# Moving one chunk's DRAM stores out of the projection stage and the first turn of the maxima forward

## The chip, the cores and the metric

The kernel runs on one core of a Trainium2 chip. The metric is device time in microseconds, the median of three runs. Engines are named as the profile names them: PE (TensorE matmul) and PEld (its weight loads), DVE (VectorE), ACT (ScalarE), POOL (GpSimd), SP (SyncE, which issues the DMAs; SPq is its queue of issues).

## The reference, cut to what matters

The whole program is two layers, each an attention-like block and an expert block. The change touches only the first block, page-masked attention on an input of 4 x 1024 tokens of width 128:

```
q = (x @ wq);  lat = x @ w_down;  k = lat @ wk_up;  v = lat @ wv_up     # 16 heads of 8
q, k = rope(q), rope(k)
scores = q . k / sqrt(8), masked to pages (32 tokens) not later than the query's
out = softmax(scores) @ v @ wo
```

Everything behind it (two expert blocks and a state-space block) is the same in both kernels.

## The kernel before, in words

Work stands in blocks. At the end of a block all engines meet, and none starts the next block before the last has arrived. Two blocks matter: `project_qkv` (line 260) and `attend` (line 505).

`project_qkv` goes over 8 chunks of 512 tokens (4 batches, `CPB` = 2 chunks each). For each chunk PE projects, DVE rotates, and ACT, POOL and DVE split the rotated q and k into three bf16 parts in the tile `parts`, which has two turns. SP then writes them to DRAM as six DMAs (line 294), behind waits on `part_ready`. Each store counts up `written[k]`. From batch 1 on, SP also issues five row loads behind each chunk's stores (line 499, through `load_rows`): the first 25 (`ROWS_BEGUN`) of the 72 loads that fill a ring of four head groups. At the end SP waits for all stores to have landed (line 304).

`attend` works on 16 groups of 4 heads; four groups belong to one batch. A group needs 18 row loads (`ROW_DMAS`), numbered n, so that n = 0 to 17 are group 0's, 18 to 35 group 1's, and so on. For each group:

- PE computes 18 blocks of scores for the row maxima (`maxima(m)`, line 747, `NI` = 18 a group), into two pairs of PSUM banks. DVE reduces each (`take(m)`, line 638), and `maxima(m)` waits for `take(m - 2)`. After a group's last one DVE combines them (lines 650 and 651).
- POOL negates the maxima and splits them into three parts (`negate`, lines 597 to 602).
- PE turns them (`turn`, line 755), ACT copies them to SBUF (line 697), and SP copies them into rows of `qr` (`neg_in_rows`, two DMAs, line 546).
- PE computes the scores with these rows in place (`scores`, line 769), ACT takes the exponent (line 714), and PE multiplies with the values (`values`, line 788).

The maxima run ahead of the scores by `LEAD` blocks. Before the loop PE issues `LEAD` maxima with nothing between them but `turn(0)`; then each of 18 steps of a group issues one maxima block, one pair of scores and the value pieces that are due. `turn(i + 1)` stands in step 14 of group i. `LEAD` was 26, and `turn(0)` stood behind 25 maxima (m = 24).

SP's order in `attend` is a list written by hand: loads n = 25 to 35, then `neg_in_rows(0)`, then loads n = 36 to 71, then `neg_in_rows(1)`, then for each later group its 18 loads, its stores and `neg_in_rows`. The sequencer takes them strictly in this order.

Of the kernel before, what the change touches and what calls it, by code (L numbers as in the profile page):

```python
# [10 lines left out]
BF16 = mybir.dt.bfloat16  # L11
# [4 lines left out]
P = 128  # L16
E = 128
B, T = 4, 1024
N = B * T
NT = N // P  # L20
CH = 512
NCH = N // CH
TPC = CH // P
CPB = T // CH
BANK = 512

H, D = 16, 8
GH = 4
# [226 lines left out]
    return q  # L255


def project_qkv(nc, g, q):

    with ExitStack() as ctx:  # L260
        sb = lambda name, shape, dt=F32: ctx.enter_context(nc.sbuf_tensor(f"qkv_{name}", shape, dt))
        sem = lambda name: ctx.enter_context(nc.semaphore(f"qkv_{name}"))
# [2 lines left out]
        latT = sb("latT", [LAT, 2, CH])  # L265
        by_cos, by_sin, rest = (sb(n, [P, 2, CH]) for n in ("by_cos", "by_sin", "rest"))
        rot = sb("rot", [P, 2, 2, CH])
        parts = sb("parts", [P, 2, 3, 2, CH], BF16)
        lat_done, lat_stored, qk_done, swap_done, v_done, v_stored = map(sem, (
            "lat_done", "lat_stored", "qk_done", "swap_done", "v_done", "v_stored"))  # L270
        cos_taken, swap_taken, rotated, rest_ready = map(sem, ("cos_taken", "swap_taken", "rotated", "rest_ready"))
        part_ready = [sem(f"part_ready{part}") for part in range(3)]
        written = [sem(f"written{k}") for k in range(2)]
        block = ctx.enter_context(nc.Block())
        WRITES = 2 * 3 * 16

        @block.sync
        def _(sp):
            for k in range(2):
                sp.sem_inc(written[k], WRITES)  # L280
            for r in range(2):

                at = HROWS * r + ROWS_QK
                sp.dma_start(g.kr[at:at + 3 + PPB, :, :, :].rearrange("r s p t -> r (s p) t"),
                             g.w["page_k"].rearrange("r (a t) -> r a t", a=1).to_broadcast([3 + PPB, RING * GP, T])).then_inc(g.masks_in, 16)
                sp.dma_start(g.qr[at + 3:at + 3 + PPB, :, :, :].rearrange("r s p t -> r (s p) t"),
                             g.w["page_q"].rearrange("r (a t) -> r a t", a=1).to_broadcast([PPB, RING * GP, T])).then_inc(g.masks_in, 16)
            begun = 0
            for b in range(B):
                for k in range(CPB):  # L290
                    for part in range(3):
                        sp.wait_ge(part_ready[part], part // 2 + CPB * b + k + 1)
                        for which in range(2):
                            sp.dma_start(g.qk_parts[which, part, b * H // GH:(b + 1) * H // GH, :, :, k * CH:(k + 1) * CH].rearrange("g d h t -> (g d h) t"),
                                         parts[:, k, part, which, :]).then_inc(written[k], 16)
                    if CPB * b + k == CPB:
                        for half in range(CPB):
                            sp.wait_ge(written[half], 2 * WRITES)
                    for n in range(begun, min(ROWS_BEGUN, begun + ROWS_A_CHUNK) if b > 0 else 0):
                        load_rows(sp, g, n // ROW_DMAS, n % ROW_DMAS)  # L300
                        begun = n + 1
            assert begun == ROWS_BEGUN
            for k in range(2):
                sp.wait_ge(written[k], WRITES + B * WRITES)

        @block.tensor
        def _(pe):
# [62 lines left out]
        def _(act):  # L370
# [8 lines left out]
            def split(b, k):  # L379
                c = CPB * b + k  # L380
                act.wait_ge(written[k], b * WRITES + WRITES)
                act.wait_ge(rotated, 1 + c + 1)
# [38 lines left out]
GP = GH // 2  # L421
NK = 9
NI = GP * NK
LEAD = NI + 8

# [61 lines left out]
def load_rows(eng, g, i, n):  # L489

    r, run = n % 2, n // 2
    if run == len(ROW_RUNS):
        at = HROWS * r + ROWS_QK
        ins = eng.dma_start(g.qr[at:at + 3, i % RING, :, :], g.w["zero_rows"].rearrange("r (p t) -> r p t", p=GP))
    else:
        which, part, first, count = ROW_RUNS[run]
        at, dst = HROWS * r + first * D, (g.qr, g.kr)[which]
        src = g.qk_parts[which, part, i:i + 1, :, :, :].rearrange("a d (p r) t -> a d p r t", r=2)[:, :, :, r, :]
        ins = eng.dma_start(dst[at:at + count * D, i % RING, :, :], src.to_broadcast([count, D, GP, T]))
    ins.then_inc(g.rows_in[i % RING], 16)  # L500


def attend(nc, g, f):

    with ExitStack() as ctx:
        sb = lambda name, shape, dt=F32: ctx.enter_context(nc.sbuf_tensor(f"att_{name}", shape, dt))
        sem = lambda name: ctx.enter_context(nc.semaphore(f"att_{name}"))
# [28 lines left out]
        @block.sync  # L536
        def _(sp):
            def store(i):
                sp.wait_ge(out_stored, i + 1)
                sp.dma_start(g.heads[GH * i:GH * (i + 1), :, :, :].rearrange("h k r t -> (h k r) t"), out_sb[:, i % 2, :]).then_inc(out_written[i % 2], 16)  # L540

            def neg_in_rows(i):
                sp.wait_ge(neg_stored, i + 1)
                for r in range(2):
                    at, rows_of = HROWS * r + ROWS_QK, 3 * GP * NJ
                    sp.dma_start(qr[at:at + 3, i % RING, :, :].rearrange("r p t -> r (p t)"),
                                 neg_rows[rows_of * r:rows_of * (r + 1), :]).then_inc(neg_in, 16)

            for n in range(ROWS_BEGUN, RING * ROW_DMAS):
                load_rows(sp, g, n // ROW_DMAS, n % ROW_DMAS)  # L550
                if n == 2 * ROW_DMAS - 1:
                    neg_in_rows(0)
            for i in range(NG):
                if i >= 1 and i + RING - 1 < NG:
                    sp.wait_ge(scores_done, UNITS * i)
                    for n in range(ROW_DMAS):
                        load_rows(sp, g, i + RING - 1, n)
                if i == LOADS_AT:
                    sp.dma_start(f.wo[:, :], g.w["wo"]).then_inc(f.wo_in, 16)
                    for group in (f.e.route, f.e):  # L560
                        for dst, src in group.pairs:
                            sp.dma_start(dst, src).then_inc(group.loaded, 16)
                if i == NG - 1:
                    f.store_inverses(sp, 2)
                    f.load_heads(sp, 2)
                if i >= 1:
                    store(i - 1)
                for b in range(3):
                    if i == SUMS_AT[b]:
                        f.load_sums(sp, b)  # L570
                for b in range(EARLY):
                    if i == INVERSES_AT[b]:
                        f.store_inverses(sp, b)
                    if i == HEADS_AT[b]:
                        f.load_heads(sp, b)
                if i < NG - 1:
                    neg_in_rows(i + 1)
            f.store_row_tables(sp, 0)
            store(NG - 1)
# [152 lines left out]
        def _(pe):  # L732
# [3 lines left out]
            def maxima(m):  # L736

                i, (pair, item) = m // NI, divmod(m % NI, NK)
                if m % NI == 0:
                    pe.wait_ge(rows_in[i % RING], ROW_LOADS * (i // RING + 1))  # L740
                if m >= 2:
                    pe.wait_ge(max_taken, m - 1)
                at = 0
                for q_block, key, n, diagonal in MAXIMA[item][0]:
                    count = ROWS_D if diagonal else ROWS_QK
                    for r in range(2):
                        last = pe.matmul(PS[:, MAX_BANK + 2 * (m % 2) + r, at:at + n], rows(qr, count, i, pair, r, q_block * P, P),  # L747
                                         rows(kr, count, i, pair, r, key, n), start=True, stop=True)
                    at += n
                last.then_inc(max_scores_done, 1)  # L750
# [40 lines left out]

            for m in range(LEAD):
                maxima(m)
                if m == LEAD - 2:
                    turn(0)
            for i in range(NG):
                for k in range(NK):
                    for pair in range(GP):
                        ahead = LEAD + NI * i + GP * k + pair
                        if ahead < NG * NI:  # L800
# [652 lines left out]
def attention(nc, g, q, f):  # L1453

    with ExitStack() as ctx:
        g.V = ctx.enter_context(nc.sbuf_tensor("V", [P, B * 4, T // P, 32], F32))
        g.qr, g.kr = (ctx.enter_context(nc.sbuf_tensor(n, [P, RING, GP, T], BF16)) for n in ("qr", "kr"))
        g.masks_in = ctx.enter_context(nc.semaphore("masks_in"))
        g.rows_in = [ctx.enter_context(nc.semaphore(f"rows_in{r}")) for r in range(RING)]
        project_qkv(nc, g, q)  # L1460
        attend(nc, g, f)
# [831 lines left out]
```

## Time and profile before

| | |
|---|---|
| median of three runs | 1396.83 us (1396.3 to 1397.82) |
| the profiled execution: time, span | 1397.44 us, 1395.6 us |
| mean granted TensorE clock | 0.937 of full |
| PE busy | 1230.7 us (88%) |
| DVE busy | 1090.8 us (78%) |
| ACT busy | 851.2 us (61%) |
| POOL busy | 574.8 us (41%) |
| `project_qkv` | about 28 to 92 us of the span |
| `attend` | about 92 to 499 us of the span |

The profile is of one execution, whose time is 0.6 us above the median and 1.8 us above its own span. Times in the rows are microseconds from the start of the span; "idle before" and its releaser stand in brackets. Matmuls are pipelined and their ends are modelled, so starts are the safer reading.

### The profile page before, as it was taken

How to read it: one execution, taken by the hardware profiler on the slowest of the kernel's cores; microseconds unless marked ns; L12 is line 12 of the kernel's file. 1: busy time of each engine (PE TensorE's matmuls, PEld its weight loads, DVE VectorE, ACT ScalarE, POOL GpSimd, SP SyncE). 2: the span in 40 equal slices, each digit the busy share in tenths (PEclk: the TensorE clock that was granted, in tenths of full speed). 3: DMA queues.
4: the chain of work that ended last, by engine and by line, in shares of the span. 5: the costliest groups of instructions: out<-in, count | busy, mean ns of one | idle time of the engine just before them, and what ended most of it. 6: DMA issues, size and time to landing. Idle time of an engine off the chain costs nothing. (4 is left out here: it accounts for less than half of the span.)

```text
span 1395.6 us, 23364 instructions
## 1 busy us (share of the span) xinstructions
PE 1230.7 (88%) x8438; PEld 643.8 (46%) x8438; DVE 1090.8 (78%) x1318; ACT 851.2 (61%) x1506; POOL 574.8 (41%) x428
## 2 busy tenths in 40 slices
PE   4936999999899989989996866999999999976998
PEld 2411333334333434444543334555555556564665
DVE  5768999989799555867455766999999999864554
ACT  2523899989799742222222678989999899512221
POOL 2320010000100236656665114888888888820000
PEclk9965999999999999999997897999999999985999
DMA  4331111311211165323361001223232223101231
GB/s 111 113 115 31 55 60 48 104 56 55 75 54 50 41 93 143 114 91 113 103 116 23 0 5 49 93 94 100 91 103 94 91 94 103 61 29 24 60 62 38
DMA packets 70525, 103.16 MB, mean 74 GB/s; under 512 B 12598, under 2 KB 42246, under 8 KB 70422
## 3 DMA queue, kind: packets, MB, share of 16 engines
q1 hardware_dynamic: 69126, 100.47, 25.1%
q10 hardware_dynamic: 1296, 1.33, 0.4%
q8 instruction: 64, 1.05, 0.3%
q14 instruction: 39, 0.32, 0.1%
HBM read 88.00 MB, written 13.37 MB: 73 GB/s over the span
## 5 line engine op out<-in xcount | busy, mean ns | idle before, releaser
L638 DVE TENSOR_REDUCE att_found<-PS 128x2 f32<-128x1024 f32 (+2 forms) x288 | 333.2, 1218 | 20.9 <-PE PS L747 19.0
L714 ACT ACTIVATE att_prob<-PS 128x512 f32<-128x512 f32 x576 | 313.6, 596 | 46.1 <-PE PS L769 34.4
L1930 POOL TENSOR_TENSOR ms_ch<-xnT,ms_c_rows 128x1024 f32<-128x1024 f32 x103 | 243.7, 2367 | 45.4 <-PE PS L1840 33.3
L1840 PE MATMUL PS<-ms_ch,ident_sb 128*128 128x512 f32 x512 | 241.2, 593 | 1.0 <-POOL ms_ch L1930 1.0
L1891 DVE TENSOR_TENSOR_SCAN xnT<-xnT,PS 128x1024 f32<-128x1024 f32 x103 | 231.0, 2267 | 7.2 <-PE PS L1831 7.1
L1869 ACT ACTIVATE ms_scaled<-m_dtu_turns,m_bt 128x256 f32<-128x256 f32 x448 | 191.6, 495 | 29.3 <-PE PS L1831 29.3
L788 PE MATMUL PS<-att_prob,att_v 128*32 128x256 f32 (+1 forms) x2560 | 185.0, 376 | 2.8 <-ACT fr_out L703 2.6
L1831 PEld LDWEIGHTS PS<-ident_sb,ms_scaled 128*128 128x128 f32 x1024 | 119.3, 142 | 81.4 <-DVE xnT L1891 37.9
L747 PE MATMUL PS<-kr,qr 55*128 55x128 bf16 (+4 forms) x1152 | 121.7, 293 | 31.0 <-PEq L260 15.8
L1831 PE MATMUL PS<-ident_sb,ms_scaled 128*128 128x128 f32 x1024 | 135.4, 276 | 11.1 <-ACT ms_scaled L1869 5.6
L1262 ACT ACTIVATE f_h<-PS,e_w_b 128x512 f32<-128x512 f32 x64 | 44.0, 687 | 140.1 <-PE PS L1413 136.9
L769 PE MATMUL PS<-qr,kr 55*128 55x128 bf16 (+4 forms) x1152 | 115.6, 279 | 15.7 <-ACT att_prob L714 8.3
L1840 PEld LDWEIGHTS PS<-ms_ch,ident_sb 128*128 128x128 f32 x512 | 87.3, 190 | 64.6 <-issue 61.2
L1876 ACT ACTIVATE xnT<-m_dt,m_a 128x1024 f32<-128x1024 f32 x103 | 116.9, 1136 | 0.0
L747 PEld LDWEIGHTS PS<-kr,qr 48*128 48x128 bf16 (+1 forms) x1152 | 39.8, 97 | 138.7 <-issue 90.6
L1243 POOL TENSOR_TENSOR f_yT<-f_yT,f_prod 128x512 f32<-128x512 f32 x56 | 71.0, 1267 | 71.6 <-DVE f_prod L1355 70.3
L1345 DVE SCALAR_TENSOR_TENSOR f_x3s<-PS,e_w_b,f_mask_row 128x512 f32<-128x512 f32 x64 | 48.0, 749 | 61.5 <-PE PS L1417 60.8
L1231 POOL TENSOR_TENSOR f_xm<-xnT,f_gate_row 128x512 f32<-128x512 f32 x64 | 81.2, 1269 | 15.7 <-DMA f_gate_row<-gate_rows_dram 14.0
L788 PEld LDWEIGHTS PS<-att_prob,att_v 128*32 128x32 f32 x2560 | 55.2, 109 | 63.2 <-issue 53.9
L1422 PE MATMUL PS<-f_h,e_w_w 128*128 128x512 f32 x128 | 67.1, 606 | 8.5 <-DVE f_prod L1355 8.4
L1413 PE MATMUL PS<-f_xm,e_w_w 128*128 128x512 f32 x128 | 68.2, 615 | 5.7 <-POOL f_xm L1231 5.7
L2165 ACT ACTIVATE f_sg<-PS 128x512 f32<-128x512 f32 x40 | 23.9, 597 | 78.7 <-PE PS L2148 78.7
(225 smaller groups left out, 1724.9 us busy)
## 6 DMA issues: line engine op xcount, KB each, us to landing
ms_c_rows<-bc_rows_dram SPq DMA_DIRECT2D x64, 512.0 KB, 3.7
f_gate_row<-gate_rows_dram SPq DMA_DIRECT2D x64, 256.0 KB, 3.5
f_mask_row<-mask_rows_dram SPq DMA_DIRECT2D x64, 128.0 KB, 3.1
qk_parts_dram<-qkv_parts SPq DMA_DIRECT2D x48, 128.0 KB, 1.9
heads_dram<-fr_out SPq DMA_DIRECT2D x16, 256.0 KB, 3.0
f_mask_row<-mask_rows_dram SPq DMA_DIRECT2D x64, 64.0 KB, 3.2
qr<-qk_parts_dram SPq DMA_DIRECT2D x32, 96.0 KB
qr<-qk_parts_dram SPq DMA_DIRECT2D x96, 32.0 KB
```

What stands on the lines that cost most here:

```text
L638: dve.tensor_reduce(found[:, :, pair, first:first + (n - 1) * step + 1:step], PS[:, bank:bank + 2, :].rearrange("p r (w n) -> p r w n", w= ...
L714: act.activation(prob[:, step % PROB_RING * GH + h, :], PS[:, SCORE_BANK + unit % SCORE_RING, :], ACT.Exp, scale=float(D) ** -0.5).then_in ...
L747: last = pe.matmul(PS[:, MAX_BANK + 2 * (m % 2) + r, at:at + n], rows(qr, count, i, pair, r, q_block * P, P), rows(kr, count, i, pair, r, ...
L769: last[r] = pe.matmul(PS[:, SCORE_BANK + (unit + r) % SCORE_RING, col:col + w], rows(kr, count, i, pair, r, j * P, P), rows(qr, count, i, ...
L788: last = pe.matmul(PS[VW * h:VW * (h + 1), VALUE_BANK, q - half * CH:q - half * CH + w], v1[:, i % 2, half, h, j, :], prob[:, step % PROB_ ...
L1231: pool.tensor_tensor(xm[:, e % XM_RING, :], xnT[:, c * CH:(c + 1) * CH], gate_row[:, e % ROW_RING, :], ALU.mult).then_inc(xm_ready, 1)
L1831: last = pe.transpose(PS[:, X_BANK + 2 * half + k // TPC, k % TPC * P:(k % TPC + 1) * P], scaled[:, s % 2, k, half, :], g.ident[:, :])
L1840: last = pe.matmul(PS[:, Y_BANK + 2 * half + q, :], g.ident[:, :], ch[:, half, q * CH:(q + 1) * CH], start=n == 0, stop=n == NS - 1)
L1869: last = act.activation(scaled[:, s % 2, i, :, :], m.dtu_turns[:, TB * b + i, :, :], ACT.Identity, scale=m.bt[:, at:at + 1])
L1876: act.activation(decay_then_h(s, half), m.dt[:, half, sequence(b)], ACT.Exp, scale=m.a[:, half, n:n + 1]).then_inc(decay_ready, 1)
L1891: dve.tensor_tensor_scan(decay_then_h(s, half), decay_then_h(s, half), inputs(half), 0.0, ALU.mult, ALU.add).then_inc(scanned, 1)
L1930: pool.tensor_tensor(ch[:, half, :], decay_then_h(s, half), c_rows[:, s % C_RING, :], ALU.mult).then_inc(ch_ready, 1)
```

## The change

The last chunk's six stores leave `project_qkv`. They are issued in `attend`, by SP, behind load n = 35 and ahead of `neg_in_rows(0)`. The wait for all stores moves to SP's place ahead of the loads of group 4 (the first of batch 1). For that, `parts` and two sets of semaphores now live through both blocks. Second, `turn(0)` stands behind 21 maxima (m = 20) in place of 25, and `LEAD` is 24 in place of 26.

```
+WRITES = 2 * 3 * 16
+def write_parts(queue, g, b, k):
+    for part in range(3):
+        queue.wait_ge(g.part_ready[part], part // 2 + CPB * b + k + 1)
+        for which in range(2):
+            queue.dma_start(g.qk_parts[which, part, b * H // GH:(b + 1) * H // GH, :, :, k * CH:(k + 1) * CH].rearrange("g d h t -> (g d h) t"),
+                            g.parts[:, k, part, which, :]).then_inc(g.written[k], 16)
 # project_qkv, SP
-                    for part in range(3):
-                        sp.wait_ge(part_ready[part], part // 2 + CPB * b + k + 1)
-                        for which in range(2):
-                            sp.dma_start(...).then_inc(written[k], 16)
+                    if CPB * b + k < NCH - 1:
+                        write_parts(sp, g, b, k)
-            for k in range(2):
-                sp.wait_ge(written[k], WRITES + B * WRITES)
 # attend
-LEAD = NI + 8
+LEAD = NI + 6
 # attend, SP
                 if n == 2 * ROW_DMAS - 1:
+                    write_parts(sp, g, B - 1, CPB - 1)
                     neg_in_rows(0)
             for i in range(NG):
                 if i >= 1 and i + RING - 1 < NG:
                     sp.wait_ge(scores_done, UNITS * i)
+                    if i == 1:
+                        for k in range(CPB):
+                            sp.wait_ge(g.written[k], WRITES + B * WRITES)
 # attend, PE
             for m in range(LEAD):
                 maxima(m)
-                if m == LEAD - 2:
+                if m == NI + 2:
                     turn(0)
```

## Rows read from the trace of the kernel before

**Rows 1.** Timeline, all engines, 76 to 93 us: start, length, what, idle before
```profile
77.84 0.75 SPq L494 DMA_DIRECT2D qr<-zero_rows  x2
...
83.53 3.49 SPq L499 DMA_DIRECT2D qr<-qk_parts_dram  x5
83.57 1.22 DVE L350 TENSOR_TENSOR qkv_parts<-qkv_rest,qkv_parts 128x1024 bf16<-128x1024 f32 x1 [4.24 <-ACT qkv_parts L388]
87.07 2.88 SPq L294 DMA_DIRECT2D qk_parts_dram<-qkv_parts  x6
91.84 0.66 SPq L499 DMA_DIRECT2D qr<-qk_parts_dram  x1
...
92.04 1.04 PE L747 MATMUL PS<-kr,qr 48*128 48x384 bf16 x8 [15.81 <-PEq L260]
```

**Rows 2.** Waits of SP's queue, 57 to 93 us: total, times, longest
```profile
SPq L304 <- DMA qk_parts_dram<-qkv_parts: 1.4, 1, 1.4
```

**Rows 3.** Timeline of the stretch before the first scores, 92 to 124 us
```profile
92.76 20.45 DVE L638 TENSOR_REDUCE att_found<-PS 128x2 f32<-128x1024 f32 x18 [0.65 <-PE PS L747]
...
114.91 0.61 PE L747 MATMUL PS<-kr,qr 48*128 48x512 bf16 x2 [1.03 <-DVE att_found L638]
114.98 0.24 POOL L602 TENSOR_TENSOR att_neg_parts<-att_neg_rest,att_neg_parts 128x32 bf16<-128x32 f32 x1
...
119.43 0.61 PE L747 MATMUL PS<-kr,qr 55*128 55x128 bf16 x6 [0.53 <-DVE att_found L638]
...
119.97 0.34 PE L755 MATMUL PS<-identb_sb,att_neg_parts 128*96 128x128 bf16 x1
...
120.65 1.56 SPq L546 DMA_DIRECT2D qr<-att_neg_rows  x2
...
122.25 5.68 SPq L499 DMA_DIRECT2D qr<-qk_parts_dram  x8
...
123.81 0.61 PE L769 MATMUL PS<-qr,kr 55*128 55x128 bf16 x4 [1.51 <-DMA qr<-att_neg_rows]
```

**Rows 4.** Timeline at the start of group 1, 144 to 150 us
```profile
144.38 0.27 ACT L697 ACTIVATE att_neg_rows<-PS 96x128 bf16<-96x128 bf16 x1
...
146.85 1.54 SPq L546 DMA_DIRECT2D qr<-att_neg_rows  x2
...
149.94 0.40 PE L769 MATMUL PS<-qr,kr 55*128 55x128 bf16 x4 [1.56 <-DMA qr<-att_neg_rows]
```

**Rows 5.** Timeline of a later group, 161 to 184 us
```profile
161.85 0.22 DVE L650 TENSOR_REDUCE att_row_max<-att_found 128x16 f32<-128x64 f32 x1
...
163.58 0.24 POOL L602 TENSOR_TENSOR att_neg_parts<-att_neg_rest,att_neg_parts 128x32 bf16<-128x32 f32 x1
...
167.31 0.26 PE L755 MATMUL PS<-identb_sb,att_neg_parts 128*96 128x128 bf16 x1
...
183.38 0.22 DVE L650 TENSOR_REDUCE att_row_max<-att_found 128x16 f32<-128x64 f32 x1
```

**Rows 6.** Timeline where the maxima end, group 14, 452 to 454 us
```profile
452.28 0.39 PE L769 MATMUL PS<-qr,kr 51*128 51x512 bf16 x2
...
453.36 0.39 PE L769 MATMUL PS<-qr,kr 55*128 55x128 bf16 x4
```

**Rows 7.** Waits of DVE over all of attention, 92 to 500 us
```profile
DVE att_found L638 <- PE PS L747: 19.0, 25, 4.9
```

**Rows 8.** Timeline of PE: two steps at 130 us, one restart at 282
```profile
129.53 1.08 PE L788 MATMUL PS<-att_prob,att_v 128*32 128x256 f32 x8
...
131.51 1.08 PE L788 MATMUL PS<-att_prob,att_v 128*32 128x256 f32 x8
...
281.71 0.61 PE L769 MATMUL PS<-qr,kr 55*128 55x128 bf16 x4 [1.66 <-DMA qr<-att_neg_rows]
```

**Rows 9.** Windows: length, busy PE, PEld, DVE, ACT, POOL, clock, DMA share, GB/s
```profile
134.00:135.00 1.00, 1.00 (x16) 0.38 (x8) 0.40 (x1) 0.68 (x2) 0.00 (x0) 0.56 0.23 74
...
284.00:286.00 2.00, 2.00 (x28) 0.69 (x30) 1.51 (x2) 1.19 (x3) 0.00 (x0) 0.73 0.19 60
```

More of the change, by code:

```diff
@@ L267, in project_qkv @@
         rot = sb("rot", [P, 2, 2, CH])
-        parts = sb("parts", [P, 2, 3, 2, CH], BF16)
+        parts, part_ready, written = g.parts, g.part_ready, g.written
         lat_done, lat_stored, qk_done, swap_done, v_done, v_stored = map(sem, (
@@ L271, in project_qkv @@
         cos_taken, swap_taken, rotated, rest_ready = map(sem, ("cos_taken", "swap_taken", "rotated", "rest_ready"))
-        part_ready = [sem(f"part_ready{part}") for part in range(3)]
-        written = [sem(f"written{k}") for k in range(2)]
         block = ctx.enter_context(nc.Block())
-        WRITES = 2 * 3 * 16
         @block.sync
@@ L290, in _ @@
                 for k in range(CPB):
-                    for part in range(3):
-                        sp.wait_ge(part_ready[part], part // 2 + CPB * b + k + 1)
-                        for which in range(2):
-                            sp.dma_start(g.qk_parts[which, part, b * H // GH:(b + 1) * H // GH, :, :, k * CH:(k + 1) * CH].rearrange("g d h t -> (g d h) t"),
-                                         parts[:, k, part, which, :]).then_inc(written[k], 16)
+                    if CPB * b + k < NCH - 1:
+                        write_parts(sp, g, b, k)
                     if CPB * b + k == CPB:
@@ L1457, in attention @@
         g.qr, g.kr = (ctx.enter_context(nc.sbuf_tensor(n, [P, RING, GP, T], BF16)) for n in ("qr", "kr"))
+        g.parts = ctx.enter_context(nc.sbuf_tensor("parts", [P, 2, 3, 2, CH], BF16))
+        g.part_ready = [ctx.enter_context(nc.semaphore(f"part_ready{part}")) for part in range(3)]
+        g.written = [ctx.enter_context(nc.semaphore(f"written{k}")) for k in range(2)]
         g.masks_in = ctx.enter_context(nc.semaphore("masks_in"))
```

## The prediction

> **What bounds the kernel now.** I read the page first: PE is busy for most of the span, and the chain that ended last lies at the far end, in the last block. So nothing there is touched, and a gain in attention counts in full only if the stages behind it simply move forward. They do, as far as they wait for attention as a whole: all engines meet at its end. So the question is what ends attention, and I went on to the timeline of the two places that the diff edits, then the waits of SP and DVE, then one group in the middle, then the clock.
>
> At the seam between projection and attention nothing computes. DVE's last work ends at 84.79 (83.57 + 1.22), SP issues five loads up to 87.02, then the last chunk's six stores up to 89.95, and attention begins at 91.84 [rows 1]. SP's wait for the landing is 1.4 us [rows 2], so that it is over at 91.35; the meeting of the engines takes the other 0.49.
>
> Before the first scores DVE sets the pace: 18 reductions in 20.45 us, one every 1.13 (17 x 1.13 + 1.23), while PE waits between its blocks [rows 3]. POOL has the negated maxima ready at 115.22 (114.98 + 0.24), but PE turns them only at 119.97, because its order puts 25 maxima ahead. SP issues the copy into the rows at 120.65, and the scores start at 123.81, having waited 1.51 for it [rows 3]. DVE needs to have done no more for this than group 0's maxima.
>
> From group 1 on, a group takes 21.53 us (183.38 - 161.85) [rows 5]. DVE's own work in it is 18 x 1.13 + 0.4 = 20.7, so PE's order sets the pace, and DVE has 0.8 to spare. One irregular place matters. At the start of group 1 the rows were copied by ACT at 144.65 (144.38 + 0.27), yet SP issues their DMAs at 146.85, since it was still busy with loads n = 36 to 71, which stand behind `neg_in_rows(0)` in its order; PE stands idle for 1.56 us until 149.94 [rows 4].
>
> **The change part by part.**
>
> *Stores out of the projection.* SP's last work there becomes the five loads that end at 87.02; every other engine is through by 84.79. With the same 0.49 for the meeting, attention begins at 87.51 in place of 91.84: 4.33 us less. Below: if the meeting is dearer when nobody has waited long, 4.0. Above, the meeting could cost nothing: 4.8. The six stores do not vanish: 2.88 us of issuing on SP behind n = 35. In attention SP issues n = 25 to 35 in about 7.2 us (eleven at 0.66 as the one in [rows 1]), to 94.7, the stores to 97.6, and then waits for the turned maxima until about 111.8. So they lie in the shade of the first maxima. Group 1's rows stand ahead of the stores, and are issued by 94.7 against their first use after 18 maxima, about 107.9. Group 0's last loads were issued at 78.59 (77.84 + 0.75) [rows 1], nine us before the new start. The new wait for the stores stands about 50 us behind their issue: nothing. Its price without that cover would be a landing, the 1.4 of [rows 2].
>
> *The turn behind m = 20.* On the axis of before, `maxima(20)` starts at 114.91 and POOL is through at 115.22 [rows 3]. Behind `maxima(24)`, PE came to the turn 0.54 after that block's start (119.43 to 119.97); the same here gives 115.45, so neither waits much for the other. That is 4.52 us earlier. SP's copy goes out 0.68 behind the turn, at 116.13 instead of 120.65, and the scores may start 3.16 behind that, at 119.29.
>
> *LEAD 24.* The block ahead of the first scores is now m = 24, which waits for DVE until 119.43 as before [rows 3]. The scores follow 0.54 later, at 119.97. So the first scores move by 3.84 us, and the copy lands 0.68 before they can use it. DVE loses its short idle time there, and so nothing is shifted onto it.
>
> *What the start of group 1 makes of it.* There SP decides, not PE. From the copy of group 0 to that of group 1 SP has 26.20 us of issuing (120.65 to 146.85), and the scores follow 3.09 after [rows 3, 4]. All of this hangs on the first copy, so group 1 starts 4.52 earlier, not 3.84: PE's idle 1.56 us shrinks to 0.88. ACT's copy would be there at 140.81, well ahead of SP at 142.33, so SP still decides. If it did not, only the 3.84 would hold.
>
> *What LEAD costs later.* Two maxima blocks leave the stretch where DVE sets the pace and go into the loop. Every step up to step 9 of group 14 issues one block as before; steps 10 and 11 of that group get one that they lacked. A step without one takes 1.08 us there (452.28 to 453.36) [rows 6], against 1.20 on average with one, turn and values included (21.53 / 18). So it costs between nothing (ACT's exponents fill most of such a step anyway) and 0.24; I take 0.1, since a plain step differs less than the mean does.
>
> *The slack of the negation.* A group's last reduction now comes two steps later, while the turn stays. Today combining starts at 161.85, POOL ends at 163.82 (163.58 + 0.24), 1.97 later, and the turn is at 167.31 [rows 5]: 3.49 to spare. Two steps are 2.26 at 1.13, so 1.2 stay. Nothing is lost, but most of the cushion is used up.
>
> Sum: 4.33 + 4.52 - 0.1 = 8.75 us. The profiled execution's span would be 1395.6 - 8.75 = 1386.85, its time 1388.7. The median of before is 0.6 below that execution, so 1396.83 - 8.75 = 1388.1.
>
> **The clock.** A cold step takes 1.98 us (129.53 to 131.51) [rows 8] at the lower level of 1.2 GHz, against the 1.20 warm: 0.39 us lost per cold us. The clock came back to 2.4 GHz late in the us 134 to 135 (mean 0.56) [rows 9], 11 us after the first scores, of which PE was dense only from 129.53. After 281.71 it came back within 3.5 us (the stretch 284 to 286 has 0.73) [rows 8, 9]. So the rise should move with the work, give or take 2 us, 0.8 us of time. Because SP sets the start of group 1, the first 0.88 us lost by PE ahead of it is free. Farther on there is luck: PE's stall of 1.66 us before 281.71 met a falling clock, the one of 1.56 before 149.94 did not. Such a fall costs about 3.5 x 0.39 = 1.4. That makes a spread of about 1.5 to both sides.
>
> The Trainium skill's page "TensorE: Matmul & The Clock Gate", Part 1, says that activity is judged in windows that run freely and don't restart with a kernel's work, so that the moment of the rise varies with where the work falls in them. The two unequal delays fit it, and it is the mechanism of the second rival.
>
> **The rivals.**
>
> 1. *Forecast*: both gains hold, 1388.1. For it: each term is a gap with a named cause. Chance 0.73, with its own range 1386.0 to 1390.0.
> 2. *The clock rises no earlier*. The rise stays at about 134.9 while the work comes 8.2 earlier. PE loses 8.2 x 0.39 = 3.2, of which 0.88 is free, so 2.3: 1390.4. Against it: the restart at 281.71. By the page's rule this is a matter of phase and would be partial. Chance 0.09.
> 3. *DVE becomes the bound*. Attention can't be shorter than DVE's chain of reductions. It idles 19.0 us over attention [rows 7] and has 0.8 us more in each group, and the forecast asks for only 2.2 less: its first reduction comes 4.33 earlier, its last 8.75 - 2.26 = 6.5. If the small slack in a group is no slack, only the 4.33 and the DVE idle time at the first scores, about 1, come: 1391.5. Chance 0.06.
> 4. *The change doesn't do what it says at the seam*: what holds attention back until 91.84 is something else, or the meeting waits for outstanding DMAs of the block by itself. Then only the 4.42 of the turn stays: 1392.4. Chance 0.05.
> 5. *Slower*: the negation misses its turn in each group, since its cushion is down to 1.2 us. PE would stand for each us that it is later, 14 times. It decides from a lateness of 1.2 + 8.75 / 14 = 1.8 us; at 2 us late, 14 x 0.8 = 11.2 is lost against 8.75 won: 1399.3. Against it: POOL's chain takes 1.97 in [rows 5], and in the first group 2.01 from the last reduction's end at 113.21 to 115.22 [rows 3]. Chance 0.03.
> 6. *Better luck with the clock*, the fall at 282 gone and the first rise early: 1386 or less. Chance 0.04.
>
> A difference under 0.2% (2.8 us) is about what can't be told from no change. Forecast, 2, 3, 4 and 6 are all faster by more than that: 0.96 with a little taken off, since a partial 4 with bad luck in the clock lands within it. Same 0.02, slower 0.03. The range from 1385.6 to 1392.0 takes in the forecast, the clock's luck on both sides and cases 2 and 3 with the spread of the runs; outside lie 4, 5 and the ends.
>
> **What the profile after would show.** The first matmul of line 747 at about 87.7; stores of line 294 (or of the new helper) on SP between 94 and 98; the first turn 23.6 us behind attention's start (before 28.1); the first scores 28.1 after it (before 32.0), without a wait for the row copy; PE's wait for `att_neg_rows` at the start of group 1 about 0.9; a group's period still 21.5; POOL's last negation 1.2 us ahead of the turn. The prediction is wrong if attention starts later than 88, if PE's turn waits for POOL in every group, or if the clock's rise does not move.

## The result, and the profile after

The changed kernel takes 1386.23 us (median of six runs, 1382.46 to 1388.82) against 1396.37 us for the kernel before in six runs (1393.34 to 1397.82): a ratio of 0.9934, interval 0.9915 to 0.9952. Forecast was 1388.1, or 8.75 us less than the 1396.83 of the first three runs; the medians of six differ by 10.1. Measured again later, the same pair gave 0.9913 (0.9887 to 0.9938). Six runs of one kernel spread over 4 to 10 us, and 35 runs of the kernel before over nearly 16, so single terms of the sum can't be read from run times. They can be read from the profiles, where the intervals inside attention that the order of issue fixes repeat to 0.1 us. The rest of the program does not repeat as well: from the end of attention to the end of the span the fourteen profiles have 890.0 to 895.9 us (895.9 and 894.7 in the first pair).

Timeline of the changed kernel at the seam (start, length, what, idle before); it answers to [rows 1]:

```profile
84.60 4.88 SPq L503 DMA_DIRECT2D qr<-qk_parts_dram  x6
84.93 1.23 DVE L354 TENSOR_TENSOR parts<-qkv_rest,parts 128x1024 bf16<-128x1024 f32 x1 [4.54 <-ACT parts L392]
88.83 0.12 POOL L591 MEMSET att_zero<- 128x32 f32 x1 [5.02 <-POOLq L272]
...
89.02 1.04 PE L755 MATMUL PS<-kr,qr 48*128 48x384 bf16 x8 [11.72 <-PEq L272]
...
96.09 2.79 SPq L266 DMA_DIRECT2D qk_parts_dram<-parts  x6
```

Attention starts 3.9 us behind the start of DVE's last work (88.83 - 84.93), before 8.28 (91.85 - 83.57). The six stores are at 96.09, in the shade of the first maxima. The group of six loads that starts at 84.60 includes the first one of attention. The fifth, the last of the projection, ends at 88.09, so the meeting of the engines takes 0.74 us here (88.83 - 88.09), where the forecast took 0.49. Everything up to here lies 1.1 to 1.4 us later than in the profile before, work that the change doesn't touch, so in what follows times are counted from attention's start.

Timeline up to the first scores, answering to [rows 3]:

```profile
89.74 20.46 DVE L646 TENSOR_REDUCE att_found<-PS 128x2 f32<-128x1024 f32 x18 [0.65 <-PE PS L755]
...
111.89 0.61 PE L755 MATMUL PS<-kr,qr 48*128 48x512 bf16 x2 [1.03 <-DVE att_found L646]
111.97 0.25 POOL L610 TENSOR_TENSOR att_neg_parts<-att_neg_rest,att_neg_parts 128x32 bf16<-128x32 f32 x1
...
112.43 0.34 PE L763 MATMUL PS<-identb_sb,att_neg_parts 128*96 128x128 bf16 x1
...
113.11 1.55 SPq L550 DMA_DIRECT2D qr<-att_neg_rows  x2
...
116.82 0.63 PE L777 MATMUL PS<-qr,kr 55*128 55x128 bf16 x4
```

The turn comes 0.54 behind its maxima block, 0.21 behind POOL's end (112.22), and 23.60 us after the start: the forecast's number. The scores start at 27.99 without a wait, forecast 28.1.

Timeline at the start of group 1, answering to [rows 4]:

```profile
138.40 0.27 ACT L705 ACTIVATE att_neg_rows<-PS 96x128 bf16<-96x128 bf16 x1
138.52 0.75 SPq L498 DMA_DIRECT2D qr<-zero_rows  x2
...
139.31 1.53 SPq L550 DMA_DIRECT2D qr<-att_neg_rows  x2
...
142.34 0.39 PE L777 MATMUL PS<-qr,kr 55*128 55x128 bf16 x4
```

The second copy goes out 26.20 us behind the first (139.31 - 113.11), as before, 4.52 us earlier counted from the start. But PE's wait for it is gone where 0.88 was forecast: the clock rose 13.3 us after the first scores and not 11.1, so PE came later. The window in which it rose (length, busy PE, PEld, DVE, ACT, POOL, clock, DMA, GB/s):

```profile
130.00:131.00 1.00, 1.00 (x16) 0.26 (x14) 0.83 (x1) 0.50 (x2) 0.00 (x0) 0.94 0.34 74
```

A later group, timelines of DVE, POOL and PE, answering to [rows 5]:

```profile
178.04 0.22 DVE L658 TENSOR_REDUCE att_row_max<-att_found 128x16 f32<-128x64 f32 x1
...
179.79 0.25 POOL L610 TENSOR_TENSOR att_neg_parts<-att_neg_rest,att_neg_parts 128x32 bf16<-128x32 f32 x1
...
181.25 0.26 PE L763 MATMUL PS<-identb_sb,att_neg_parts 128*96 128x128 bf16 x1
...
199.57 0.22 DVE L658 TENSOR_REDUCE att_row_max<-att_found 128x16 f32<-128x64 f32 x1
```

A group still takes 21.53, and POOL ends 1.21 us ahead of the turn, where the forecast said 1.2.

Attention as a whole took 402.01 us, from 88.83 to the first load of the expert block at 490.84; before, 407.83. That is 5.8 less, and the forecast had 4.4. The first profile pair shows one place that was not forecast. PE's wait of 1.66 us at the start of group 7, at whose end the clock fell [rows 8, 9], is down to a quarter of a microsecond:

```profile
272.26 0.39 PE L777 MATMUL PS<-qr,kr 55*128 55x128 bf16 x4 [0.24 <-DMA qr<-att_neg_rows]
```

From the copy for group 7 to that for group 8 it is 24.49 us before and 21.04 after. The other way, the last group of the changed kernel met a clock at half speed from about 461 to 471. Behind its last row copy attention takes 40.8 us, in the kernel before 38.4, so this cost some 2.4 us. Whether such places belong to a kernel or to one execution, one pair of profiles can't tell.

### The profile page after: what moved, and what is told of

It reads as the page before. It is cut to its first block and busy times, and to the rows that moved or that the text cites. A ratio compares the mean times of both kernels' runs of the same rounds, so it can differ in the third digit from the quotient of the medians.

```text
span 1385.5 us, 23363 instructions
## 1 busy us (share of the span) xinstructions
PE 1233.7 (89%) x8438; PEld 647.1 (47%) x8438; DVE 1089.5 (79%) x1318; ACT 851.2 (61%) x1506; POOL 575.9 (42%) x428
## 3 DMA queue, kind: packets, MB, share of 16 engines
q8 instruction: 64, 1.05, 0.3%
## 5 line engine op out<-in xcount | busy, mean ns | idle before, releaser
L777 PE MATMUL PS<-qr,kr 55*128 55x128 bf16 (+4 forms) x1152 | 116.0, 279 | 10.3 <-ACT att_prob L722 7.4
L1239 POOL TENSOR_TENSOR f_xm<-xnT,f_gate_row 128x512 f32<-128x512 f32 x64 | 81.2, 1271 | 11.4 <-DMA f_gate_row<-gate_rows_dram 7.5
L605 POOL TENSOR_TENSOR att_neg<-att_zero,att_row_max 128x32 f32<-128x32 f32 x16 | 4.1, 254 | 164.7 <-DVE att_row_max L659 164.7
```

Of the source, the lines that this page charges most:

```text
L777: last[r] = pe.matmul(PS[:, SCORE_BANK + (unit + r) % SCORE_RING, col:col + w], rows(kr, count, i, pair, r, j * P, P), rows(qr, count, i, ...
L1239: pool.tensor_tensor(xm[:, e % XM_RING, :], xnT[:, c * CH:(c + 1) * CH], gate_row[:, e % ROW_RING, :], ALU.mult).then_inc(xm_ready, 1)
```

## The experiments

Eight further kernels ran, and four of the ten were run once more. The table gives what thirteen of the profiles show, in us; that of e5_lead22 is told under its run. Seam: from the start of DVE's last work in the projection to attention's start. First turn, first scores, copy 0 and copy 1 (the row copies of groups 0 and 1) are counted from attention's start. Wait: PE's wait for copy 1. Rise: from the first scores to the return of the clock to 2.4 GHz. Length: of attention, to the first load of the expert block.

| kernel | seam | turn | scores | copy 0 | copy 1 | wait | rise | length |
|---|---|---|---|---|---|---|---|---|
| before | 8.28 | 28.1 | 32.0 | 28.80 | 55.00 | 1.56 | 11.1 | 407.83 |
| b_again | 8.19 | 28.1 | 31.9 | 28.80 | 55.01 | 2.67 | 8.9 | 407.96 |
| e1_stores_only | 4.08 | 28.2 | 31.9 | 28.84 | 55.06 | 2.42 | 9.3 | 407.58 |
| e3_lead_only | 7.89 | 25.9 | 29.6 | 26.53 | 52.74 | 2.01 | 10.3 | 404.43 |
| e4_turn_only | 6.84 | 23.6 | 30.2 | 24.27 | 50.87 | none | 10.4 | 401.82 |
| e2_turn_lead_only | 7.95 | 23.6 | 28.0 | 24.27 | 50.48 | 0.88 | 11.5 | 400.53 |
| after | 3.90 | 23.6 | 28.0 | 24.28 | 50.48 | none | 13.3 | 402.01 |
| a_again | 3.72 | 23.6 | 28.0 | 24.28 | 50.50 | 1.97 | 8.9 | 401.37 |
| e6_rows20 | 1.51 | 23.6 | 28.0 | 24.27 | 50.67 | none | 15.2 | 400.47 |
| e6_again | 1.52 | 23.6 | 28.0 | 24.27 | 50.50 | 0.94 | 11.4 | 400.39 |
| e7_copy_ahead | 4.41 | 23.6 | 28.0 | 24.28 | 50.70 | none | 15.3 | 403.90 |
| e8_both | 1.51 | 23.6 | 28.0 | 24.28 | 48.25 | 0.68 | 9.5 | 401.41 |
| e8_again | 1.52 | 23.6 | 28.0 | 24.28 | 49.87 | none | 13.3 | 399.86 |

### One half of the change at a time

**e1_stores_only**, the changed kernel with the old lead and the old place of the turn:

```
-LEAD = NI + 6
+LEAD = NI + 8
-                if m == NI + 2:
+                if m == LEAD - 2:
                     turn(0)
```

> Only the last chunk's stores are moved (LEAD 26, first turn behind m = 24, as before). Two separate gaps: attention begins 4.1 to 4.4 us sooner behind the projection's last DVE work (before: 8.27 us behind its start, now 3.9), nothing changes inside attention: first turn 28.1 us and first scores 32.0 us after attention's start, 1.5 us idle for the row copy at the start of group 1. Time 4.3 us under before (1392). Rival, one gap gives the room for the other (part of the gain is only there with both): under 3 us or over 6 us. If the stall of 1.7 us at the start of group 7 depends on the order of maxima, it is still there in this kernel; if it is a matter of how the weight loads fall, it may be there or not.

Measured: 1390.2 us (12 runs), ratio 0.997 (0.9949 to 0.9991) to the kernel before on its chip, 3.7 us less by the medians. The seam is 4.08 and attention as long as before. So the seam's gain stands alone. The start of group 7 waited for only 0.22 us here, with LEAD 26. PE's timeline at the start of group 1, and the clock behind it:

```profile
147.36 0.50 PE L777 MATMUL PS<-qr,kr 55*128 55x128 bf16 x4 [2.42 <-DMA qr<-att_neg_rows]
```

```profile
147.00:148.00 1.00, 0.64 (x8) 0.31 (x12) 0.00 (x0) 0.06 (x1) 0.00 (x0) 0.76 0.11 41
148.00:149.00 1.00, 1.00 (x10) 0.13 (x4) 0.00 (x0) 1.00 (x2) 0.00 (x0) 0.50 0.23 74
```

The clock had risen early here (9.3), PE then waited longer, 2.42 us, and the clock fell behind the wait.

**e2_turn_lead_only**, the kernel before with the other half:

```
-LEAD = NI + 8
+LEAD = NI + 6
-                if m == LEAD - 2:
+                if m == NI + 2:
                     turn(0)
```

> Only the turn and the lead are changed; the stores stay in the projection. Separate gaps: attention begins as before (8.3 us behind the start of DVE's last work), the first turn comes 23.6 us and the first scores 28.0 us after attention's start, group 1's scores 53.6 us after it (before 58.1), time 4.4 us under before (1392). If LEAD 24 also takes away the stall of 1.7 us at the start of group 7 and the fall of the clock behind it, attention is shorter by 5.8 us as in the changed kernel, and the time is 5.8 under (1390.5). Rival, DVE bound: under 1.5 us.

Measured: 1388.92 us (12 runs), ratio 0.9965 (0.995 to 0.9981), 5.0 us less. Turn, scores and copy 1 are as in the changed kernel to 0.02 us, group 1's scores come 53.62 us after the start, forecast 53.6. Attention is 7.3 us shorter than in the first profile of the kernel before. DVE is not the bound. e1's and e2's ratios leave 0.3% and 0.35%, and the whole change 0.66% and 0.87% in its two measurements: the halves add up within what the runs can tell.

**e3_lead_only**, the kernel before with `LEAD = NI + 6` and the turn still behind `LEAD - 2`:

> Only LEAD is 24; the first turn stands behind m = 22 by the old rule LEAD - 2. The turn comes two reductions sooner, 25.9 us after attention's start, the scores 3.8 us behind it, 29.7, with about 1.5 us idle for the row copy, and group 1's scores 2.3 us sooner: 2.2 us under before (1394.2). If the stall at group 7 goes away by LEAD alone, it is absent here and the time is about 3.6 under (1392.8).

Measured: 1391.24 us (12 runs), ratio 0.9978 (0.9962 to 0.9994), 2.7 us less. Turn 25.86, scores 29.63, copy 1 2.27 us sooner than before, as expected; attention is 3.1 to 3.5 us shorter. The expectation asked whether LEAD alone takes the wait at group 7 away: it is still there with 1.12 us, but without a fall of the clock.

**e4_turn_only**, the kernel before with the turn behind `m == NI + 2` and LEAD still 26:

> Only the first turn is put behind m = 20; LEAD stays 26. The turn comes 23.6 us after attention's start, but the scores stand behind m = 26, which waits for DVE: 30.4 us after the start (1.6 sooner). Group 1's scores come 3.1 us sooner, since SP's row copy no longer holds them. Time 3.1 us under before (1393.3). Rival, what counts is when the scores begin, and SP's loads don't matter: 1.6 us. The stall at group 7 is there as before if it depends on the order of maxima.

Measured: 1389.93 us (12 runs), ratio 0.9974 (0.9955 to 0.9994), 4.0 us less. The turn is at 23.60 and the scores at 30.24 (expected 30.4). The interval between the copies is 26.60 here, more than SP's 26.20, so PE and ACT set it, and PE does not wait at all for the copy. Group 1's scores come 54.44 us after the start (147.54 - 93.10), 3.65 sooner than before, where 3.1 was expected. Attention is 401.82 us long, 6.0 under the first profile. The rest of that is not the turn's doing: the first profile had no fall of the clock at group 1, but one at group 7, and from copy 6 to copy 8 it has 47.10 us against 44.75 here. Against b_again and e1 it is the fall at group 1 that is gone with the wait: from copy 1 to copy 2 they have 23.92 and 22.51, e4 21.53. In what the order of issue fixes, the first turn alone brings 3.65 of the 4.5 us that turn and lead bring together.

### How much room the lead has

**e5_lead22**, the changed kernel with `LEAD = NI + 4`:

> The changed kernel with LEAD 22 in place of 24. Theory, the cushion of 1.2 us between POOL's last negation and the turn is what limits LEAD: the last reduction of a group comes 2.26 us later still, so the turn stands 1.05 to 1.2 us for POOL in each of 14 groups, a group takes 22.6 us in place of 21.5, and the time is some 13 to 16 us over the changed kernel (about 1400). Rival, there is more room (DVE is ahead there, or PE's waiting is won back by its next steps): within 2 us of the changed kernel.

Measured: 1424.19 us (6 runs), ratio 1.0199 (1.0172 to 1.0226) to before. The changed kernel was not measured beside it; at its two ratios it would take 1382 to 1385 us, so this is some 40 us over it. The direction is that of the theory (13 to 16 us over), the size nearly three times its own. DVE's timeline of two combinings, PE's at the turn between them, and two windows of the clock behind the turn:

```profile
234.34 0.22 DVE L658 TENSOR_REDUCE att_row_max<-att_found 128x16 f32<-128x64 f32 x1
...
236.47 0.23 PE L763 MATMUL PS<-identb_sb,att_neg_parts 128*96 128x128 bf16 x1 [1.51 <-POOL att_neg_parts L610]
...
258.87 0.22 DVE L658 TENSOR_REDUCE att_row_max<-att_found 128x16 f32<-128x64 f32 x1
```

```profile
238.00:239.00 1.00, 1.00 (x16) 0.57 (x16) 0.74 (x2) 0.66 (x2) 0.00 (x0) 0.63 0.05 12
239.00:240.00 1.00, 1.00 (x18) 0.58 (x18) 0.77 (x1) 0.97 (x2) 0.00 (x0) 0.50 0.14 29
```

PE stands for POOL's negation for 1.51 us in each group, and a group takes 24.53 us in place of 21.53. The expectation had the wait at 1.05 to 1.2. Another 1.5 us go with the clock, which falls behind the wait. Two steps of lead fewer turn a cushion of 1.21 us into a loss of 3.0 us per group.

### Two steps further

**e6_rows20**, the changed kernel with the last five row loads taken out of the projection too:

```
-ROWS_BEGUN = ROWS_A_CHUNK * (NCH - CPB - 1)
+ROWS_BEGUN = ROWS_A_CHUNK * (NCH - CPB - 2)
```

> The changed kernel, and the five row loads n = 20 to 24 leave the projection too (ROWS_BEGUN 20). Theory, what ends the projection now is only SP's list: then the next in line is DVE's last work, and attention begins 1.7 to 2.0 us behind that work's start in place of 3.9, 2 us sooner; inside attention nothing changes, since SP's list of 16 loads and 6 stores (about 13.6 us) still ends before the first copy at 24.3. Time 2 us under the changed kernel. Rival, the meeting of the engines or a landing holds it at 3.9: no gain. Rival, group 1's loads come too late for the 19th maxima block (21 us after the start): a stall of DVE there.

Measured: 1383.81 us (6 runs), ratio 0.9927 (0.9902 to 0.9952) to before on its chip. Timeline at the seam:

```profile
84.26 1.23 DVE L354 TENSOR_TENSOR parts<-qkv_rest,parts 128x1024 bf16<-128x1024 f32 x1 [4.40 <-ACT parts L392]
85.76 4.20 SPq L503 DMA_DIRECT2D qr<-qk_parts_dram  x6
85.77 0.12 POOL L591 MEMSET att_zero<- 128x32 f32 x1 [2.63 <-POOLq L272]
...
85.96 1.03 PE L755 MATMUL PS<-kr,qr 48*128 48x384 bf16 x8 [9.19 <-PEq L272]
```

DVE's last work ends at 85.49, and attention starts 0.28 behind it. Inside attention the first turn, the first scores and copy 0 didn't move.

**e7_copy_ahead**, the changed kernel with the copy of group 1 ahead of SP's last four loads:

```
                     neg_in_rows(0)
+                if n == RING * ROW_DMAS - 5:
+                    neg_in_rows(1)
...
-                if i < NG - 1:
+                if 0 < i < NG - 1:
                     neg_in_rows(i + 1)
```

> The changed kernel, and SP issues the row copy of group 1 ahead of the last four of the loads n = 36 to 71. Theory, SP's list sets the start of group 1 (26.20 us from the first copy to the second in five kernels of this study): the copy now goes out as soon as ACT has it or 2.9 us sooner, whichever is later; with the clock's rise as in the changed kernel that is 0.6 us sooner, with an early rise up to 1.5. So the interval shrinks from 26.20 to between 23.3 and 25.8, and the time by 0.5 to 1.5 us. Rival, the interval is set by PE and ACT: nothing.

Measured: 1385.11 us (6 runs), ratio 0.9927 (0.99 to 0.9954). The changed kernel was not measured beside it, and the profile doesn't decide: the clock rose 15.3 us after the first scores, and SP stood for ACT's copy, so that the interval was 26.42 us.

**e8_both**, both edits:

> Both of these edits on top of the changed kernel: rows n = 20 to 24 moved and the copy of group 1 ahead of four loads. Separate gaps: 2 us from the seam and 0.5 to 1.5 at the start of group 1, 2.5 to 3.5 us under the changed kernel (about 1383 against 1386 on the same chip), attention's start 1.7 to 2.0 behind the start of DVE's last work in the projection.

Measured: 1381.84 us (6 runs), ratio 0.9906 (0.9879 to 0.9934). With an early rise (9.5) the interval between the copies is 23.97 us, so SP's list is what had set 26.20. But the scores gain less, as SP's and PE's timelines show:

```profile
134.73 1.48 SPq L550 DMA_DIRECT2D qr<-att_neg_rows  x2
...
139.03 0.39 PE L779 MATMUL PS<-qr,kr 55*128 55x128 bf16 x4 [0.68 <-DMA qr<-att_neg_rows]
```

The scores follow 4.30 us behind the issue of the copy, where it was 3.03 to 3.16 in the rows above. Why this landing is later was not tried. It is not peculiar to e8: at group 7 the scores follow the issue of the copy by 5.08 us in the first profile of the kernel before and by 4.43 in e4, PE waiting for the landing both times.

### The same kernels again, on one chip

**a_again**, **b_again**, **e6_again** and **e8_again** are the changed kernel, the kernel before, e6_rows20 and e8_both without an edit.

> The changed kernel once more, for its time beside the two below on one chip and for a second profile. Inside attention the first turn 23.6 us, the first scores 28.0 and the second row copy 50.5 us after the start are fixed by the order of issue and come out again within 0.1; what follows the clock may differ: its rise 9 to 15 us after the first scores, and the wait for the row copy at group 7 between 0 and 2 us. If the long wait at group 7 in the kernel before (1.66 us, with a fall of the clock, 3.1 us in all) is chance, the median gain over many runs is near 8.7 us and not the 10 of the two profiles.

> The kernel before once more, for a second profile. First turn 28.1, first scores 32.0, second row copy 55.0 us after attention's start again; attention begins 7 to 8.3 us behind the start of DVE's last work in the projection. If group 7's long wait was chance, the interval between its row copies is now about 21.1 to 22.5 in place of 24.5, and attention 3 us shorter than in the first profile. If it belongs to the kernel, 24.5 comes again.

> The kernel with five more row loads out of the projection (ROWS_BEGUN 20), beside the changed kernel on one chip: attention's start again 1.5 us behind the start of DVE's last work (3.9 to 4.4 in the changed kernel), the time 2.4 us less.

> Both edits, beside the changed kernel on one chip: 2.4 us from the seam, and at the start of group 1 between 0 and 1.5 us, since the first look showed the copy going out at 24.0 us behind the first in place of 26.2, but PE still waiting 0.7 us for it. Time 2.4 to 3.5 us less than the changed kernel.

Measured against 1394.9 us for the kernel before: a_again 1384.28 (0.9913, 0.9887 to 0.9938), b_again 1393.12 (0.9994, 0.9975 to 1.0014), e6_again 1380.6 (0.9898, 0.987 to 0.9926), e8_again 1382.38 (0.9901, 0.9876 to 0.9926). Everything that the order of issue fixes came again within 0.1 us, the seam within 0.2. Copy 1 of e6 and e8 is not of that kind: where the clock rose late SP stood for ACT's copy, and e8 has 48.25 and 49.87. The gain of the changed kernel did not shrink to the 8.7 us that a_again expected: the medians differ by 10.6. e8_again is 1.9 us under the changed kernel, where 2.4 to 3.5 was expected.

Group 7 was chance: b_again shows 21.49 us between the copies for groups 7 and 8 where the first profile had 24.49. But b_again is no shorter than the first profile, since its PE waited 2.67 us at group 1 and the clock fell at the end of that wait. The interval from copy 1 to copy 2 was 23.92 us, against 21.06 in the first profile.

The profiles also show what the chance is. SP's list sets the start of group 7 too, since the weight loads for later blocks stand in it ahead of that group's row copy. From the first of them (`fr_wo`) to the copy SP took 7.2 to 9.0 us, because one or two of these loads, mostly done in 0.5, held it longer, a single one for up to 3.4. In the nine profiles with LEAD 24 PE's wait follows this length: none at 7.23 to 7.36, 0.24 and 0.34 at 7.66 and 7.55, then 0.73 at 8.09, 0.91 at 8.29, 1.12 at 8.50 and 1.60 at 8.99. That last one is e8_both, in which the clock fell at group 7 as it had in the kernel before. SP's timeline of its three `e_w_sw` loads:

```profile
261.06 4.29 SPq L572 DMA_DIRECT2D e_w_sw<-sw  x3
```

In the kernel before the list was short (7.47), and the wait of 1.66 came from the late landing told above.

The order of maxima does matter in one way, which all profiles of the table agree on. At group 6, DVE has 0.95 us of another work, the reciprocal that divides batch 0, right behind a combining. PE's wait for DVE there, in the kernel before:

```profile
271.96 0.39 PE L747 MATMUL PS<-kr,qr 48*128 48x512 bf16 x2 [0.72 <-DVE att_found L638]
```

and in the changed kernel:

```profile
266.62 0.39 PE L755 MATMUL PS<-kr,qr 48*128 48x512 bf16 x2 [0.32 <-DVE att_found L646]
```

With LEAD 26 it is 0.72 or 0.73 (before, b_again, e1, e4), with LEAD 24 0.32 or 0.33 (all others). From copy 6 to copy 8, less the wait at group 7, it is 43.8 to 44.0 us with LEAD 26 (b_again, e1, e4) and 43.4 to 43.6 in the eight profiles with LEAD 24 in which the clock did not fall there.

The reciprocal of batch 1, in group 10, shows the same 0.72 and 0.32, but a few microseconds on PE stands much longer, in every profile of the table, for 4.2 to 5.4 us. In the kernel before:

```profile
370.59 0.31 PE L755 MATMUL PS<-identb_sb,att_neg_parts 128*96 128x128 bf16 x1 [4.60 <-POOL att_neg_parts L602]
```

POOL negates late here because it first divides batch 0, and that waits for the DMA into `fr_inv` (until 365.28); the clock is down there for 3.4 to 10.2 us. The change leaves this place as it was, and no run here tried it.

e6 is the fastest in the median on the last chip, 3.7 us under the changed kernel, and 2.2 us of that are the seam (3.72 to 1.52). The intervals of e6, e8 and the changed kernel overlap, so only the profiles, not the times, say that e6 is faster; between e6 and e8 nothing is decided.

## Why the prediction was right

**The seam.** Forecast 4.33. In five profiles with the stores in the projection the seam is 6.84 to 8.28 (mean 7.83), in five that differ from the changed kernel only inside attention (e1, e5, e7 and its own two) 3.72 to 4.41 (mean 4.06): 3.8 us, and 4.4 in the first pair. e1 shows that it comes from the stores alone, and e6 that the five loads were next in line, as the forecast had read them. The fourth rival (something else holds the start) is out. The meeting of the engines is not one number: it costs 0.28 where DVE came last (e6) and 0.74 where SP did (the changed kernel), and the forecast took 0.49. By its letter one of the forecast's signs of being wrong came true, since attention starts at 88.83, later than 88. But DVE's last work starts 1.36 later in that profile, and counted from it the start is at 3.90, forecast 3.94.

**The turn and the lead.** Forecast: turn at 23.6, scores at 28.1, copy 0 4.52 earlier, copy 1 26.20 behind it. All came out within 0.15 us in the changed kernel's profiles. That SP's list sets the start of group 1 and not PE is shown by three things: 26.20 to 26.23 in every profile in which PE waited for the copy and the list was not changed, longer intervals (26.40, 26.42, 26.60) where PE was late and did not wait, and 23.97 with the list changed. What SP issues ahead of the first copy costs nothing: even in e6, with 16 loads and six stores, it ends at 99.34 and the copy goes out at 110.04.

**What was mis-sized.** Attention became 6.8 us shorter in the mean, not 4.4: the three profiles with the old turn and lead have 407.58 to 407.96 (mean 407.8), the five of after, a_again, e2, e6 and e6_again 400.39 to 402.01 (mean 401.0). Split at the row copies, the means differ by 4.5 us up to copy 1, by 1.0 from copy 1 to copy 2 and by 1.4 from copy 6 to copy 8. Two more differences cancel, 0.6 less from copy 10 to copy 12 and 0.7 more behind copy 15; both lie at falls of the clock, and no run ties them to the change.

The 1.0 is the fall of the clock at the wait of group 1. The forecast counted the wait only, as 1.56 going to 0.88, and left falls of the clock to luck. But an early rise makes the wait long, and a wait of 1.97 or more went with a fall in all four profiles that had one (b_again, e1, e3, a_again), one of 1.56 or less with none at this place. From copy 1 to copy 2 these old and new kernels have 21.0 to 21.5 without a fall and 22.5 to 23.9 with one, in line with the 1.4 that the forecast took for a fall (b_again has twice that, its clock stayed down twice as long). Two of the three old kernels' profiles had it, one of the five new ones. That the change makes such falls rarer follows from the shorter wait, but eight profiles don't show how much.

Of the 1.4, some 0.4 is LEAD: forecast as a cost of 0.1, it is a gain of 0.4 at the place of the reciprocal (0.72 to 0.32). By the rows, the combining and the reciprocal now fall in a step in which PE has 16 value matmuls to do in place of eight; that this is the reason is argued, not tried. In the stretch where the maxima end nothing was lost: from copy 14 to 15 it is 23.00 and 23.03. What is left, about 1 us, is chance, the wait and fall at group 7 in one of the three old profiles, 3.1 us spread over three.

So the sum 8.75 was made of a seam taken 0.5 too large and terms inside attention taken some 2.4 too small. Seam and attention together give 10.6 (3.8 + 6.8), and the two measured differences are 10.1 and 10.6. About 1 us of the profiles' 6.8 is the luck told above, so they explain the medians to about that much and no better. A slip without effect: the chances of the faster cases add up to 0.97, where the forecast writes 0.96.

**The rivals.** The clock did rise late in the changed kernel's first profile, 13.3 us after the scores, 2.2 more than before. But it rose earlier than in the profile before, at 130.1 against 134.9, so it moved with the work in part. The loss of 2.2 x 0.39 = 0.86 us lay under SP's list, as the forecast had said of the first 0.88; PE came at the very moment when the copy landed. DVE as the bound is refuted by e2. The slower rival was right in its mechanism and its cushion (1.21 us), and e5 shows it with two steps of lead fewer; but its price was taken at 1 us per us late. Measured is 3.0 us per group for a wait of 1.51, so it would have decided at half the lateness beyond the cushion.

**Open.** Why the copy landed later in e8, what sets the rise between 8.9 and 15.3 us, and why one weight load held SP for up to 3.4 us.

## What to carry to other kernels

When a queue issues a hand-written list, find the list's length between two steps that others wait for: here 26.20 us from one row copy to the next, and so every microsecond at the head of the list was one at the start of group 1, as long as PE got there before the copy had landed. At a meeting of all engines, list who arrives when, and move what has only the last arrival behind it and is not needed at once; then look who is next (stores, then loads, then DVE's own work). A lead in a ring is worth cutting only down to the cushion of the slowest chain that hangs on it; compute that cushion first (3.49 - 2 x 1.13 = 1.2 us), since one more cut of the same size made the kernel 30 us slower than before, some 40 us slower than with LEAD 24.

## What the runs showed of the hardware

The return of TensorE's clock from 1.2 to 2.4 GHz came 8.9 to 15.3 us after the same instruction in thirteen profiles with nearly the same work ahead of it. It is not fixed to the work: the two profiles of the changed kernel have 13.3 and 8.9. That agrees with the Trainium skill, "TensorE: Matmul & The Clock Gate", Part 1, that the judging of activity runs freely. It does not agree in size: the page gives a variation of 500 ns to each side, here the spread is 6.4 us. That is also wider than the 2 us to each side that the forecast allowed.

A short wait of PE in dense work can cost twice. With waits of 1.97 to 2.42 us at group 1 came 3.4 us at 1.2 GHz, with the one of 2.67 6.8 us, and in e5 a wait of 1.51 in each group cost as much again in time. At group 7 the waits of 1.66 (before) and 1.60 (e8_both) went with a fall, those of 1.12 and less did not, nor did the wait of 1.56 in [rows 4]. Between 1.5 and 1.7 us both happened.
